# The low part of h in the merged light and routing stage, made by POOL between its bias additions instead of by DVE

## What is computed

```python
x = x + _L1_ffn_ref(x, routing_token, light_..., heavy_...)

def _L1_ffn_ref(...):
    light_out = feed_forward(x, light_gamma, light_w1, light_b1, light_w2, light_b2)
    s = einsum('bnd,d->bn', x, routing_token)
    scores = coor_descent(s, effective_k, 50, 1.0)     # 50 rounds of a, b
    sel_scores, sel_idx = top_k(scores, 512)
    ...
def feed_forward(x, gamma, w1, b1, w2, b2):
    h = gelu(rms_norm(x, gamma) @ w1 + b1)
    return h @ w2 + b2
```

## Time and profile before

| | before |
|---|---|
| median of 3 runs | 3937.42 us (3932.35 to 3938.48) |
| profiled execution, its own time | 3931.68 us |
| its span | 3930.0 us |
| granted TensorE clock, mean | 0.947 of 2.4 GHz |
| PE busy | 3518.3 us, 90% |
| DVE busy | 2744.7 us, 70% |
| POOL busy | 1921.5 us, 49% |
| ACT busy | 1506.5 us, 38% |
| DVE operations of L1733, first and last start | 3223.4 and 3484.6 us |

### The profile page before, as it was taken

How to read it: one execution, slowest core, us unless ns; L and a number is a source line. 1 busy time by engine, 2 the same in 40 slices (tenths; PEclk the granted TensorE clock), 3 DMA queues, 4 the chain that set the end, 5 groups by cost and what they waited for, 6 DMA issues and landing times. The chain is left out here.

```text
span 3930.0 us, 55737 instructions
## 1 busy us (share of the span) xinstructions
PE 3518.3 (90%) x16111; PEld 2376.0 (60%) x16111; DVE 2744.7 (70%) x5462; ACT 1506.5 (38%) x5254; POOL 1921.5 (49%) x1789
## 2 busy tenths in 40 slices
PE   8599999999946799999999599999999958879998
PEld 4355555555525677777777355555555536657776
DVE  3477777777669676776767367777777758766665
ACT  0256666666610111111111166666666634211110
POOL 0255555555510567677776355555565633223322
PEclk9799999999975899999999799999999979989999
DMA  5454555555420566666666444654654447521101
GB/s 162 134 146 139 144 161 141 144 156 146 119 76 11 156 162 163 161 165 169 155 173 149 109 133 134 172 146 133 169 153 141 131 147 273 188 97 22 18 12 14
DMA packets 323310, 523.14 MB, mean 133 GB/s; under 512 B 59352, under 2 KB 104216, under 8 KB 322648
## 3 DMA queue, kind: packets, MB, share of 16 engines
q1 hardware_dynamic: 290904, 443.79, 37.9%
q0 software_dynamic: 32256, 77.65, 10.4%
HBM read 283.64 MB, written 136.96 MB: 107 GB/s over the span
## 5 line engine op out<-in xcount | busy, mean ns | idle before, releaser
L691 ACT ACTIVATE t_pr<-ps,t_negmax 128x154 f32<-128x154 f32 x2048 | 867.8, 547 | 530.8 <-DVE t_negmax L471 530.4
L414 POOL TENSOR_TENSOR t_pr<-t_pr,t_inv 128x616 f32<-128x616 f32 x512 | 639.8, 1251 | 620.7 <-DVE t_inv L486 618.1
L494 DVE COPY t_pTm<-ps 128x512 f32<-128x512 f32 x512 | 350.0, 684 | 316.7 <-PE ps L735 312.6
L785 PE MATMUL ps<-t_xnT,t_wq 128*128 128x512 f32 x1024 | 506.2, 618 | 19.4 <-ACT t_qT L612 19.1
L806 PE MATMUL ps<-t_wo,t_oT 128*128 128x512 f32 x1024 | 501.1, 613 | 7.6 <-DVE t_xs L503 6.5
L734 PEld LDWEIGHTS ps<-ident,t_pr 128*128 128x128 f32 x2048 | 318.2, 204 | 295.6 <-issue 262.5
L691 ACT ACTIVATION_READ_ACCUMULATOR t_pr<-ps,t_negmax 128x1 f32 x2048 | 471.8, 230 | 0.0
L471 DVE TENSOR_REDUCE t_negmax<-ps 128x4 f32<-128x616 f32 x512 | 403.1, 787 | 28.5 <-PE ps L722 28.0
L734 PE MATMUL ps<-ident,t_pr 128*128 128x128 f32 x2048 | 334.2, 286 | 51.2 <-DVE t_pTm L494 37.6
L722 PE MATMUL ps<-t_kst,t_stack 98*128 98x154 f32 x2048 | 340.0, 289 | 13.4 <-DMA t_stack<-t_q_low 13.0
L785 PEld LDWEIGHTS ps<-t_xnT,t_wq 128*128 128x128 f32 x1024 | 176.9, 192 | 230.1 <-issue 203.4
(11 more groups left out here) (297 smaller groups left out, 7297.0 us busy)
## 6 DMA issues: line engine op xcount, KB each, us to landing
t_stack<-t_q_high SPq DMA_DIRECT2D x1024, 64.0 KB, 2.1
e_wgu_in<-in_gate_upT SPq DMA_DIRECT2D x32, 1536.0 KB, 6.6
t_stack<-t_q_low SPq DMA_DIRECT2D x512, 64.0 KB, 2.0
x_dram<-t_xs SPq DMA_DIRECT2D x32, 1024.0 KB, 5.6
t_kst<-kst_dram SPq DMA_DIRECT2D x128, 235.8 KB
e_wd_in<-in_downT SPq DMA_DIRECT2D x32, 768.0 KB
xs_dram<-t_z SPq DMA_DIRECT2D x16, 1032.0 KB
l_z<-xs_dram SPq DMA_DIRECT2D x16, 1032.0 KB
```

The source lines that it names most:

```text
L414: pool.tensor_tensor(p, p, inv[:, v, :].unsqueeze(1).to_broadcast([P, KEYS, HG]), ALU.mult).then_inc(s["normed"], 1)
L494: dve.tensor_copy(pTm[:, g % 2, :, t * P:(t + 1) * P], ps[:, 4, :].rearrange("p (h n) -> p h n", h=HG)).then_inc(s["pTm"], 1)
L691: op = act.activation(pr[:, u % 4, :, h], ps[:, 2 * (u % 2) + h // 2, at:at + KEYS], ACT.Exp, bias=negmax[:, u, h:h + 1], accum_out=total[ ...
L785: mm = pe.matmul(ps[:, A_BANK, :], wq[:, k, n * P:(n + 1) * P], xnT[:, k, :], start=(k == 0), stop=(k == DC - 1))
```

## The change

`split_h` leaves DVE's queue and comes to POOL's. POOL's loop per group was a wait for xs and four bias additions. It is now: low part of h for f = 0, bias of tile 1, low part for f = 1, bias of tiles 2 and 3, and then, ahead of the next group's low part, the wait for the next xs and its bias of tile 0. The number of routing steps between the remaining operations of DVE is unchanged.

```diff
-            for n in range(NG):
+
+            def with_bias(n, tiles):
                 q = n % 2
                 pool.wait_ge(s[f"xs_in{q}"], 16 * (n // 2 + 1))
-                for t in range(TG):
+                for t in tiles:
                     pool.tensor_tensor(xs[q][:, t, :], xs[q][:, t, :], b2[:], ALU.add).then_inc(s["xb2"], 1)
+
+            def split_h(n, f):
+                pool.wait_ge(s["h_high"], LC * n + f + 1)
+                pool.tensor_tensor(hT[1][:, f, :], h[:, f, :], hT[0][:, f, :].bitcast(F32),
+                                   ALU.subtract).then_inc(s["hT"], 1)
+
+            with_bias(0, (0,))
+            for n in range(NG):
+                split_h(n, 0)
+                with_bias(n, (1,))
+                split_h(n, 1)
+                with_bias(n, (2, 3))
+                if n + 1 < NG:
+                    with_bias(n + 1, (0,))
...
-            def split_h(n, f):
-                dve.wait_ge(s["h_high"], LC * n + f + 1)
-                dve.tensor_tensor(hT[1][:, f, :], h[:, f, :], hT[0][:, f, :].bitcast(F32),
-                                  ALU.subtract).then_inc(s["hT"], 1)
-
...
                 advance(pace[0])
-                split_h(n, 0)
                 advance(pace[1])
                 z_low(n + 1, 0)
                 advance(pace[2])
-                split_h(n, 1)
                 advance(pace[3])
                 z_low(n + 1, 1)
```

## The result

| | before | changed |
|---|---|---|
| median of 5 runs | 3933.47 us (3929.0 to 3938.48) | 3953.84 us (3948.64 to 3956.91) |
| ratio to before, 95% interval | | 1.0048 (1.0033 to 1.0062) |
| span of the profiled execution | 3930.0 us | 3946.9 us |

A forecast was written before the change was run, and what follows sets the result against it. The program was taken as nearest to TensorE, with DVE's queue ahead of result to watch; +2, +1.6 and +2.3 gave +6 us, 3937.7 on the profiled execution or 3943.4 on the median, forecast 3941, range 3928 to 3953.

The forecast's parts named there:

- rival 2: Each group loses one more POOL operation, +20 us, 3957; longer waits for result would slow TensorE further; chance 0.15.
- The conflict: Group 2: a wide operation on DVE meets POOL's bias 2, +1.0 us; result(2, 0) comes 0.5 us later.
- sbv: From group 3 on, POOL's window no longer reaches this DVE operation: -0.48 us a ring, its 1.16 us falling to a quarter.
- the rounds: Groups 0 to 6, a ring running from outer(n, 2, 0) to the next: +2 us in all, ring about 15.6 us.
- the sum: All groups of the changed stage: +2, +1.6 and +2.3 us, together +6 us.
- The hots: Group 13: four hot operations on DVE end 0.4 us behind POOL's; result(13, 0) at 3453.5 instead of 3452.59.
- POOL: Subtraction takes 1.26 to 1.4 us, 32 times; TensorE's waits for hT_low gone; xs landing has 8 us of cover.
- behind the search: Groups 11 to 15, where one-hot rows are made: four groups 2.0 us, group 15 +0.3, together +2.3 us.
- Groups 7 to 10: The search by digits: kind, cand and lower on DVE meet POOL's biases; +0.4 us each, +1.6 us in all.
- Group 0: First group of the stage: xs of group 1 has landed, POOL runs on into its bias; +1 us.
- Rival 1: The relief wins: DVE's wides or hots fall into gaps of POOL's work; -18 us, 3924, half of it 3932; chance 0.15.
- Rival 3: No effect: DVE's savings and losses land in its waits for ACT; within 2 us of zero, 3937; chance 0.2.

The follow-up runs named there:

- e5: Changed kernel with 7, 20 or 10 extra unused matmuls ahead of outer(n, 2, 0) in every group; 3936.83 us, 1.0009 to before.
- e3: Against the kernel before, only the subtractions moved to POOL, all four bias additions back behind the xs landing; 3926.62 us, ratio 0.9982.
- e4: Subtractions on POOL, three bias additions at the landing and the fourth between the subtractions; 3927.96 us, 0.9988 to the kernel before.
- e10: As e4 with 12 extra matmuls in groups 7 to 10 and the additions of groups 8 to 11 placed apart; 3920.41 us, 0.9970 to before.
- e2: Control: the kernel before with seven extra unused matmuls per group in groups 0 to 10; 3933.06 us, ratio 1.0002.
- e9: Against the kernel before, only the bias additions in their new places, subtractions still on DVE; 3954.90 us, ratio 1.0063.
- e1: Changed kernel with seven extra unused matmuls ahead of outer(n, 2, 0) in groups 0 to 10; 3947.87 us, 1.0036 to the kernel before.
- e7: Changed kernel without the 64 bias additions, b2 left out of the output; 3911.27 us, 0.9943 to the kernel before.

## Why the prediction was off in size

The forecast was +6 us, written as 3941; the kernel came out some 19 us over the kernel before (0.48% of 3933), and its median, 3953.84, 0.8 us past the upper end of the range. The case that came true is the size of rival 2 (+20), which had 0.15, and not by its first mechanism, one more conflict a group, but by the sentence at its end: a longer wait lowers TensorE's clock. The last of the prediction's own signs of being wrong, "a longer wait takes TensorE's clock down in groups that had it full", came true.

Right, step by step:
- **The conflict.** "The wide at 3258.28 meets bias 2", and +0.5 at result(2, 0): measured +0.51, with the first wide missing the gap by 0.1 us and the second running free, as worked out.
- **sbv.** It fell to 0.25 us. With the clock restored (e5) five rings of the rounds are 15.55 us each, where the sum had 15.6.
- **The hots.** z_low to result(n, 0) in the late groups was to be 5.34 us (3453.5 - 3448.16); the changed kernel's timeline has 3466.66 - 3461.34 = 5.32. The ring at full clock is 18.95 us, 18.46 before: +0.5, as predicted.
- **POOL.** 1.30 us a subtraction, TensorE's waits for hT_low gone, no new wait for the landing.
- **The sum without the clock.** e5 measured +0.09% (0.00 to 0.18%), 0 to 7 us; the sum was +6. By stretches e5 is 2.4 us over before in the rounds (+2 in the sum), 3.0 behind the search (+2.3), and 1.6 under it in the search (+1.6). The last is no test of the term, since the clock there was 0.98 against 0.94.

Wrong:
- **The missing term.** The sum priced result's delay at its own length, as if TensorE's pace were fixed: "TensorE is spared its wait for hT_low", "but then waits for result(2, 0) just the same". Just the same in time, but not in form. Waits of 0.42 us for hT_low and 1.05 us for result, with products between them, became one of 2.24 us: 0.5 by the conflict, the rest by products that now ran earlier and left the idle time in one piece. Behind it came seven matmuls at half clock, 7 x 0.2 = 1.4 us, in five of the six rings of the rounds, and about 1.3 us in the late rings (result(13, 1) to result(13, 2): 5.80 us for 4.45). The rounds, the search (5.2 us) and the late rings together are the 15 us that e5 took away. Rival 2 named it, and gave it no number, though the window of group 8 in the earlier trace rows showed 0.92 behind a long wait: the rows for a price were there.
- **Groups 7 to 10** were taken at +0.4 each, 1.6 in all. Four profiled executions have the additions in the new places and no more than seven matmuls of filler: 96.39, 97.07, 97.16 and 96.71 us, at clocks of 0.89 to 0.91. The two of the old order have 92.77 and 91.42, at 0.94. With the clock at 0.98 the new order has 91.17 (e5). So the +3.6 us there repeats, and it went with the clock; the sum had no term for it here either. How much of the conflicts' +1.6 is real isn't shown.
- **Group 0.** +1 expected. The change of kernel moved the start of the stage by 1.9 us, and first results are 0.9 us earlier by the trace, so about +1 counted from there; its 3.15 us wait is the longest of the rounds.
- **Rival 1** needed the additions out of the stretch behind h_high(n, 1). e3, e4 and e10 (this one with filler in the search) did that and are 0.12 to 0.30% faster. Its 18 us were too many: e10 is at -12 us. Rival 3 had no part.

What stays open: why the late groups of one execution run at 0.92 with waits that leave another at 1.00 (e2 against before). The experiments did not tell this apart. With it stays open how much of the +6.8 us behind the search is the change's, and how much a chance of the one profiled execution before.

## What to carry to other kernels

Before moving work to POOL, list which DVE operations run in the time in which POOL will be busy, and whether they can run beside it: a 0.24 us operation that is issued 0.1 us behind a 1.26 us POOL operation becomes 1.22 us. Here the place of POOL's other work (the additions) mattered more than the operation that was moved: with the same subtractions on POOL the kernel was 0.48% slower or 0.18% faster (e3). So place it where DVE waits anyway, or give DVE's short operations a form that doesn't conflict. And when a wait of TensorE gets longer, or two short ones merge, add the matmuls behind it at half clock to the sum; filling the wait with useless matmuls, beside a control in the old kernel, tells whether that is the cause. The length of a ring doesn't tell it: 17.0 us came once from a late result and half clock, and 17.2 us from held-up DVE operations alone at full clock (e9).

## What the runs showed that was not expected

- Matmuls that compute nothing, put into a wait, made the rings of the rounds 1.4 us shorter (e1), and the changed kernel 0.39%, some 15 us, faster when used in all groups (e5).
- The length of the wait does not decide the clock by itself: 2.24 us was followed by matmuls of 0.63 us, while outer(0, 2, 0) of the changed kernel, behind 3.15 us, ran at 0.50, in a ring at a granted clock of 1.00; and in e2 the clock was at 0.92 behind waits of 1.17 and 0.45 us.
- Without the bias additions and with the subtractions on POOL, groups 7 to 10 take 80.73 us (e7), 12 less than in the kernel before; with the additions at the landing they take 87.27 (e3).
- The same length of ring in the rounds, 17.0 and 17.2 us, had half clock in it in the changed kernel and full clock in e9.
